# Softmax division behind the value product, as rows of reciprocals, and a transposed copy shared by two engines

## What is computed

```python
q = jnp.einsum('bpd,hdk->bphk', x, W_Q)      # 32 query heads, 8 key heads, d_head 64
k = jnp.einsum('bpd,ndk->bpnk', x, W_K)
v = jnp.einsum('bpd,ndk->bpnk', x, W_V)
gq = q.reshape(b, s, n_kv, g, d_head).transpose(0, 1, 3, 2, 4)
scores = jnp.einsum('bqgnh,bknh->bnqk', gq, k) / jnp.sqrt(jnp.float32(d_head))
scores = jnp.where(causal, IGNORE, scores)
pattern = jax.nn.softmax(scores, axis=-1)
z = jnp.einsum('bknh,bnqk->bqnh', v, pattern)
attn_out = jnp.einsum('bqnh,nhd->bqd', z, W_O)
```

## Time and profile before

| | us |
|---|---|
| median of 3 runs | 589.4 (585.45 to 589.74) |
| profiled execution | 584.7 |
| its span, first to last instruction | 582.9 |
| busy in it: PE / PEld | 512.2 / 418.7 |
| DVE / ACT / POOL | 380.2 / 287.3 / 158.1 |

### The profile page before, as it was taken

The page is one execution under the profiler, slowest core; times in us unless marked ns, Lnnn a source line. Parts: engine busy times, 40 slices in busy tenths (PEclk is TensorE's granted clock), DMA queues, the critical chain, the costliest instruction groups (busy, mean ns, idle before and its releaser), DMA issues. The chain is left out here.

```text
span 582.9 us, 9925 instructions
## 1 busy us (share of the span) xinstructions
PE 512.2 (88%) x3274; PEld 418.7 (72%) x3275; DVE 380.2 (65%) x964; ACT 287.3 (49%) x528; POOL 158.1 (27%) x205
## 2 busy tenths in 40 slices
PE   1996977899999999899989999717999999999994
PEld 1645865687797875666768778617888888998883
DVE  4896577746654736777777878455777666666661
ACT  1476353223502345465466656325666666666651
POOL 3703539402002202333223212110322222222222
PEclk9999999899998996899899999957999999999999
DMA  8997001000001009600000002941122222222211
GB/s 336 394 335 221 2 18 55 1 1 0 1 2 36 1 0 396 269 27 30 28 2 28 20 10 74 403 151 28 30 37 36 36 36 36 36 36 36 27 15 22
DMA packets 25780, 47.46 MB, mean 81 GB/s; under 512 B 2192, under 2 KB 21136, under 8 KB 25360
## 3 DMA queue, kind: packets, MB, share of 16 engines
q1 hardware_dynamic: 21232, 41.35, 19.8%
q0 software_dynamic: 4080, 5.15, 6.0%
q10 hardware_dynamic: 432, 0.49, 0.3%
HBM read 32.01 MB, written 14.98 MB: 81 GB/s over the span
## 5 line engine op out<-in xcount | busy, mean ns | idle before, releaser
L1602 PE MATMUL ps<-split,xsT 128*128 128x352 f32 x552 | 95.5, 330 | 0.8 <-DVE split L1244 0.8
L1602 PEld LDWEIGHTS ps<-split,xsT 128*128 128x128 f32 x552 | 89.5, 192 | 1.0 <-issue 1.0
L1244 DVE TENSOR_TENSOR split<-early,split 128x1408 fp32r<-128x1408 f32 x46 | 72.6, 1617 | 1.9 <-ACT split L783 1.9
L1624 PE MATMUL ps<-mid,work 128*128 (+1 forms) x276 | 67.9, 388 | 0.8 <-ACT work L772 0.8
L783 ACT CAST split<-early 128x1408 fp32r x46 | 62.6, 1365 | 0.8 <-issue 0.8
L1624 PEld LDWEIGHTS ps<-mid,work 128*128 128x128 f32 (+1 forms) x276 | 49.7, 189 | 13.4 <-issue 8.7
L1225 DVE TENSOR_TENSOR work<-work,ps 128x704 f32<-128x704 f32 x23 | 20.4, 886 | 56.4 <-PE ps L1602 56.4
L1114 DVE TENSOR_REDUCE nmax<-ps 128x1 f32<-128x128 f32 (+7 forms) x64 | 45.4, 750 | 7.3 <-PE ps L1508 7.2
L564 POOL TENSOR_TENSOR rstd<-mhalf 128x1 f32<-128x1 f32 x23 | 11.4, 494 | 138.3 <-ACT work L779 138.3
L1519 PE MATMUL ps<-cst,work 128*128 128x128 f32 x216 | 35.6, 293 | 4.8 <-DVE work L1122 2.8
L728 ACT COPY work<-ps 128x128 f32<-128x128 f32 (+7 forms) x32 | 20.6, 642 | 33.9 <-PE ps L1519 33.8
(11 more groups left out here) (250 smaller groups left out, 1118.1 us busy)
## 6 DMA issues: line engine op xcount, KB each, us to landing
early<-m_w SPq DMA_DIRECT2D x16, 704.0 KB, 10.1
expert_in<-pad SPq DMA_DIRECT2D x8, 1040.0 KB, 12.6
mid<-m_w SPq DMA_DIRECT2D x8, 640.0 KB, 8.5
work<-expert_in SPq DMA_DIRECT2D x23, 130.0 KB, 2.6
early<-factors SPq DMA_DIRECT2D x1, 2048.0 KB, 12.1
early<-wq SPq DMA_DIRECT2D x1, 2048.0 KB, 16.5
mid<-f_w SPq DMA_DIRECT2D x1, 2048.0 KB, 21.3
rows<-x_in SPq DMA_DIRECT2D x2, 512.0 KB, 4.9
```

Of the source, the lines that this page charges most:

```text
L1244: V.tensor_tensor(lo, (ew1, ew3)[w][:, bass.ds(e, 1), :], hi.bitcast(F32), ALU.subtract).then_inc(s_wlo[w], 1)
L1602: last = mm(ps[:, 2 * w + a, 0:IH], xsT[px][b][:, k, :], split_w[w][pw][:, k, a * IH:(a + 1) * IH], start=(k == 0 and px == pw), stop=(k = ...
L1624: last = mm(ps[:, 6, 0:D], eaT[0:w, b, c, :], we[0:w, c, :], start=(c == 0), stop=(c == IB - 1))
```

## The change

The exponentials are no longer divided by their sum. They are transposed and multiplied by v as they are, and the attended values, feature-major, are multiplied by rows that hold the reciprocals. VectorE takes the reciprocals of a tile's eight sums, copies each over 64 columns, TensorE transposes the four blocks of 128, ScalarE copies them to SBUF, and VectorE multiplies. In tiles 0 to 3 the transposes of the two heads of a step use bank 4 and bank 5 in turn, and ScalarE copies them whole. From tile 4 (WIDE = 32 heads) a row takes both banks; ScalarE copies the first 512 columns and VectorE the others, and the transposes of a step's first head come at the end of the step in which its exponentials are made. Attention output, routing transposes, counts, the choice of experts and the slots have other places in the orders, and the two new buffers take 1024 columns below k_hi, so that fewer parts of w3 are loaded early.

```diff
+        R_AT = K_AT - 2 * QB * P
+        inv_rows = early[:, R_AT:R_AT + QB * P]
+        inv_cols = early[:, R_AT + QB * P:K_AT]
+        WIDE = GT * HEADS
+        def pT_banks(u):
+            return 4 if u >= WIDE else 4 + u % 2
 # SP
-            early_w3 = (K_AT - E * KD * I) // (KD * I)
+            early_w3 = (R_AT - E * KD * I) // (KD * I)
+            below_k = -(-(K_AT - E * KD * I) // (KD * I))
...
-            for e in range(early_w3, E):
+            for e in range(below_k, E):
...
+            sp.wait_ge(s_zT, TT)
+            for e in range(early_w3, below_k):
+                sp.dma_start(ew3[:, e], m_w3[:, e]).then_inc(s_e13, 16)
             sp.wait_ge(s_pv, TT * HEADS // 2)
 # ScalarE
             def probs_feature_major(u):
-                w = (u // HEADS + 1) * P
+                w = min((u // HEADS + 1) * P, 512)
...
-            def z_feature_major(i):
+            def reciprocal_rows(i):
+                act.wait_ge(s_inv_tr, i + 1)
...
+                nc.scalar.copy(inv_rows, ps[:, 6 + (i + 1) % 2, :]).then_inc(s_inv, 1)
-            for m in range(STEPS + 7):
+            for m in range(STEPS + 6):
                 i, rel = divmod(m, PAIRS)
-                if rel == 2 and 1 <= i <= TT:
-                    z_feature_major(i - 1)
+                wide = 2 * m > WIDE
+                if rel == 1 and i >= 2:
+                    logits_exp(i - 2)
                 if 1 <= m <= STEPS:
                     probs_feature_major(2 * m - 2)
+                if rel == 2 and 1 <= i <= TT:
+                    reciprocal_rows(i - 1)
                 if rel == 0 and i >= 2:
                     routed_feature_major(i - 2)
-                if rel == 1 and i >= 2:
-                    logits_exp(i - 2)
+                if wide and m <= STEPS:
+                    probs_feature_major(2 * m - 1)
                 if m < STEPS:
                     attend(2 * m)
+                if 1 <= m and not wide:
+                    probs_feature_major(2 * m - 1)
+                if m < STEPS:
                     attend(2 * m + 1)
-                if 1 <= m <= STEPS:
-                    probs_feature_major(2 * m - 1)
 # VectorE
-            def normalised(u):
...
+            def probs_feature_major(u):
+                w = (u // HEADS + 1) * P - 512
+                dve.wait_ge(s_pt, u + 1)
+                dve.wait_ge(s_pv, u // 2 - 1)
+                V.tensor_copy(pT[u % 4][:, 512:512 + w], ps[:, 5, 0:w]).then_inc(s_pTv, 1)
+            def reciprocals(i):
+                dve.wait_ge(s_pr, (i + 1) * HEADS)
...
+                link(V.reciprocal(pinv[:, c], psums[:, c]))
+                V.tensor_copy(inv_cols.rearrange("p (n d) -> p n d", n=HEADS),
+                              pinv[:, c].unsqueeze(2).broadcast_to([P, HEADS, DH])).then_inc(s_pinv, 1)
+            def attended_normalised(i):
+                dve.wait_ge(s_inv, i + 1)
+                dve.wait_ge(s_pv, (i + 1) * PAIRS)
...
+                V.tensor_tensor(zT.rearrange("p a b -> p (a b)"), ps[:, 6 + i % 2, :], inv_rows,
+                                ALU.mult).then_inc(s_zT, 1)
...
-            for m in range(STEPS + 7):
+            for m in range(STEPS + 6):
                 i, rel = divmod(m, PAIRS)
-                if rel == 2 and i >= 2:
-                    route_slots(i - 2)
+                wide = WIDE < 2 * m <= 2 * STEPS
+                if wide:
+                    probs_feature_major(2 * m - 2)
+                if rel == 0 and i >= 2:
+                    route_normalise(i - 2)
                 if rel == 1 and i >= 2:
-                    route_max(i - 2)
-                if 1 <= m <= STEPS:
-                    normalised(2 * m - 2)
-                    normalised(2 * m - 1)
+                    route_choice(i - 2)
+                if m < STEPS:
+                    row_max(2 * m)
+                    row_max(2 * m + 1)
+                if wide:
+                    probs_feature_major(2 * m - 1)
+                if rel == 0 and 1 <= i <= TT:
+                    reciprocals(i - 1)
+                if rel == 2 and 1 <= i <= TT:
+                    attended_normalised(i - 1)
                 if rel == 3 and 1 <= i <= TT:
                     add_attention(i - 1)
                     route_variance(i - 1)
-                if m < STEPS:
-                    row_max(2 * m)
-                    row_max(2 * m + 1)
-                if rel == 3 and 1 <= i <= TT:
-                    route_normalise(i - 1)
+                if rel == 0 and i >= 2:
+                    route_max(i - 2)
                 if rel == 1 and i >= 2:
-                    route_choice(i - 2)
                     route_tail(i - 2)
+                    route_slots(i - 2)
 # TensorE
             def probs_transposed(u):
-                pe.wait_ge(s_pn, u + 1)
-                if u >= 1:
+                pe.wait_ge(s_pr, u + 1)
+                if u >= WIDE:
                     pe.wait_ge(s_pT, u)
+                    if u > WIDE:
+                        pe.wait_ge(s_pTv, u - WIDE)
+                elif u >= 2:
+                    pe.wait_ge(s_pT, u - 1)
...
             def attended(m):
+                if 2 * m >= WIDE:
+                    pe.wait_ge(s_pTv, 2 * m + 2 - WIDE)
-                if pair == 0 and i >= 2:
-                    pe.wait_ge(s_slots, i - 1)
+                if pair == 0 and i >= 1:
+                    pe.wait_ge(s_inv, i)
...
+            def reciprocals_transposed(i):
+                pe.wait_ge(s_pinv, i + 1)
+                if i >= 1:
+                    pe.wait_ge(s_cnt_read, i)
+                for pair in range(PAIRS):
+                    last = nc.tensor.transpose(ps[:, 6 + (i + 1) % 2, pair * P:(pair + 1) * P],
+                                               inv_cols[:, pair * P:(pair + 1) * P], ident)
+                last.then_inc(s_inv_tr, 1)
...
-                if 1 <= m <= STEPS:
-                    probs_transposed(2 * m - 2)
+                if rel == 2 and 1 <= i <= TT:
+                    reciprocals_transposed(i - 1)
+                if rel == 3 and 1 <= i <= TT:
+                    attention_out(i - 1)
                 if rel == 0 and i >= 2:
                     route_transposed(i - 2)
+                if 1 <= m <= WIDE // 2:
+                    probs_transposed(2 * m - 2)
+                if 1 <= m <= STEPS:
+                    probs_transposed(2 * m - 1)
+                if rel == 1 and i >= 2:
+                    route_counts(i - 2)
                 if 2 <= m <= STEPS + 1:
                     attended(m - 2)
-                if 1 <= m <= STEPS:
-                    probs_transposed(2 * m - 1)
-                if rel == 2 and 1 <= i <= TT:
-                    attention_out(i - 1)
                 if rel == 0 and i >= 2:
                     route_logits(i - 2)
-                if rel == 1 and i >= 2:
-                    route_counts(i - 2)
+                if WIDE // 2 <= m < STEPS:
+                    probs_transposed(2 * m)
```

30 lines of the change are left out of this document (14 added, 16 removed).

## The result

| | before | after |
|---|---|---|
| median of 20 runs each, us | 589.51 (584.38 to 590.88) | 584.96 (578.95 to 591.89) |
| ratio, 95% interval | | 0.9923 (0.9896 to 0.9950) |
| profiled execution / its span | 584.7 / 582.9 | 581.0 / 579.2 |
| mean granted clock of it | 0.957 | 0.972 |

The forecast was 1.4 us slower; the kernel became about 4.5 us faster, 0.8% by the ratio. Ratios leave out the runs that are over 1.5% above the fastest of their kernel, six of these twenty of the changed kernel and none of before, while medians and means take all: the means of the twenty are 588.0 and 585.3, so the gain is 0.5% by the means.

A forecast was written before the change was run, and what follows sets the result against it. TensorE was taken as the attention stage's bound, at 92%. Stage before its tail -1.3 and tail +2.7 sum to +1.4: 586.1 us on the profiled 584.7, 590.8 on the median 589.4; range 582.5 to 597.

The forecast's parts named there:

- tile 1, "+1.2": Tile 1: no idle time to give, +0.4 or +0.9 for added transposes by clock, plus the reciprocal-row wait: +1.2 us.
- rival (2): Clock rises in tile 1, whose 14.08 us hold 8.3 of work at 2.4 GHz: up to -5.8, about 585; chance 0.12.
- of the 2.0 us that TensorE idles I give back 1.3: Tile 3, tile 2 the same: 1.3 of 2.0 us TensorE idle time returns, the rest being counts that still wait.
- the wait for the reciprocal rows: Tiles 1 to 3: a tile's first value product waits for ScalarE's copy of the reciprocal rows, 0.75 us.
- four steps at "about 0.1": Tile 4: the split copy cuts about 0.1 us a step, against 0.43 for transposes and the dearer output; taken as 0.
- the steps forecast at 6.0, 6.2 and 6.2: Tile 7's steps with routing transposes and logits (6.0 us), choice of experts (6.2) and reciprocals (6.2).
- The tail: After the last exponential: routing transposes +0.25, counts before the last value product +1.2, reciprocals and product behind it +1.3; together +2.7.
- SP's late loads: Two of eight w3 loads move behind the last normalised values; costed at nothing, 1 to 4 us if stores queue behind.
- a rival at +2 to +4: Late w3 loads do collide: +2 to +4 us, 593 to 595; chance 0.08.
- The fifth rival: VectorE's part is slower still, maxima and PSUM copies in one queue, 0.2 in each of 16 steps: +3.2, 594; chance 0.07.
- The first, all waits gone: TensorE never waits in the attention stage: -6.9 us, 582.5; chance 0.15.
- The third, low clock through tiles 2 and 3: Clock stays at 1.2 GHz through tile 2 or 3 too; one more such tile costs 5.8 us, 596.6; chance 0.13.

The follow-up runs named there:

- after_held: Changed kernel with tile 0's old wait put back: VectorE takes an unread reciprocal, scales rows by 1.0, transposes wait for it; 593.58 us, ratio to before 1.0058.
- before_filler: Kernel before plus thirteen unread 256-column matmuls, 9 and 4 around the first transposes of tile 0; 581.14 us, ratio 0.9900.
- no_norm: Kernel before without the division: no reciprocals or scalings, transposes wait for the exponentials alone, output not the softmax; 583.15 us, ratio 0.9883.
- ao_later: Changed kernel with the attention output placed behind the second head's transposes; one run, tiles 3 to 6 shorter by 0.51, 0.44, 0.41 and 0.30 us.
- tail: Changed kernel, reordered behind the last exponential: reciprocal transposes before the last value product, tile 6's counts after it, VectorE's product before the slots; 587.44 us, ratio 0.9868.
- tail_loads: Kernel tail with other homes for the two new buffers and tile 6's store no longer ahead of the late w3 loads; 584.06 us, ratio to before 0.9864.
- whole_copy: Changed kernel with ScalarE copying the whole transposed row in tiles 4 to 7; one run, tiles 4, 5, 6 longer by 0.30, 0.72 and 0.90 us.
- after_filler: Changed kernel plus unread 256-column matmuls where TensorE stands, 4 in tile 0 and the others in the tail and before the experts; 582.16 us.

## Why the prediction was wrong

**The step that failed** is tile 1, "+1.2", and behind it the weight of rival (2). The sum took tile 1 to be at 1.2 GHz as before, and the trace of the kernel after shows 1.00 and 10.28 us: -3.8. The median by rival (2) was to be "about 585", and it is 584.96. I gave it 0.12. That the two agree so well is luck: the rival took 5.8 us off tile 1, the trace 3.8, and twelve of the twenty runs have more low clock than the traced one. The prediction named the fact that pointed to it, the 1.22 and 0.45 us for which TensorE stood in tile 0 just ahead of the fall, and costed the removal of that stand at its own length only. after_held and before_filler show the link from both sides. no_norm does not settle which part of the change matters: with VectorE's wait gone, but the 0.45 behind ScalarE's copy still there, the clock fell, but it fell as well in ao_later, tail and tail_loads, which have the changed tile 0, and all four traces had the lower clock ahead of attention. Whether the two banks in tile 0 matter beside the division is open; the banks alone were not tried. Even in the changed kernel twelve of twenty runs have more low clock than the eight best. The gain is thus one of odds. 46.8 us of low clock on the mean against some 60 are 13 x 0.315 = 4.2 us, less 1.8 of structure: -2.4. The means of the 20 runs each are 588.0 and 585.3, a difference of 2.7. The 4.5 between the medians is more than that because of where each lies in its upper group.

**The structure, at equal clock.** before_filler gives the tiles of before at full clock, so the terms can be laid side by side: tile 0 -1.2 (forecast -1.2), tile 1 +0.6 (+1.2), tile 2 +0.5 (-0.1), tile 3 +0.7 (-0.1), tile 4 -1.2 (0; in part clock, see below), tile 5 -0.6 (-0.3), tile 6 -0.4 (-0.4), tile 7 -0.3 (-0.4). Together -1.9, where -1.3 was forecast; without the clock's part in tile 4 it is an estimated -0.5. Misses of both signs partly cancel.

- Tiles 2 and 3: "of the 2.0 us that TensorE idles I give back 1.3" was wrong. The counts still wait 1.0 and 0.7 us there, and 1.05 us of wait before the first wide scores (ScalarE puts a copy between the two exponentials that they need, at 264.28) was not seen. That wait could have been read off the diff: the last narrow step has the narrow order, but the scores behind it already want wide banks.
- Tile 1: the wait for the reciprocal rows is 0.8 as forecast (0.75), but the prediction added the doubled cost of the transposes at 1.2 GHz.
- Tile 4: both traces of the order before have 3.4 us at 1.2 GHz in it, and no_norm, at full clock, took 19.93. With the 0.4 to 0.6 that the division costs in the tiles beside it, tile 4 of before would be some 20.4 at full clock, an estimate; then the changed order is 0.3 longer there and the clock accounts for about 1.5. whole_copy gives the split copy 0.3 in the tile; four steps at "about 0.1" were to be 0.4.
- Tiles 5 to 7 came out as worked: 5.88, 6.23 and 6.30 us for the steps forecast at 6.0, 6.2 and 6.2. VectorE's copy of 512 columns takes 0.69 us, the value taken from L1110, and releases the second transposes. The rule of the Trainium skill weighed there (VectorE: DVE Perf Modes, section "Why PSUM operands drop a tier"), that a PSUM operand costs VectorE its fast pass, fits: 688 ns for 512 columns from PSUM, beside 753 for 1024 in SBUF. It did not decide, since whole_copy shows the split to gain 2.6 us all the same; the freed ScalarE pays for it.

**The tail** was forecast at +2.9 from the last exponential to the residual add (13.9 against 11.03) and measured at +4.3, 1.2 of it the clock. Order and places were right: a last value product behind the counts with 2.2 us of wait (forecast "some 2"), then transposes, copy and product. Up to the first expert product it is +3.8, where the sum had +2.7. The stage's -0.5 and these 3.8, less the 1.2 of clock, make 2.1, near the 1.8 found at equal clock.

**SP's late loads** were costed at nothing, with a rival at +2 to +4. In the changed kernel they are just level with the table; once the tail is shorter they take its whole gain, as tail shows. The sum over stages hides this: two chains end at the experts, and shortening one of them alone gives nothing.

**The fifth rival**, a slower VectorE, is out by the steps of tile 7. The first, all waits gone, is out by the counts. The third, low clock through tiles 2 and 3 for the stand ahead of the value product, is not seen: in every trace with the changed orders tile 2 is at 0.90 or more and tile 3 at 1.00.

## What to carry to other kernels

Where the trace shows TensorE at 1.2 GHz in a full stretch, read what it did just before, and price a removed or added stand there by the tile that follows as well as by its own length: here 1.22 us of standing went with 4.4 us in the next tile. Look at the low clock of every run before trusting a median, since it can sit at the edge of one of two groups, and compare orders at equal clock; one trace of a kernel can show the good case alone. When a chain is shortened, ask which other chain ends at the same place; here the transfers for the next stage and then the first rows behind the table.

## What the runs showed of the hardware

- Fifty to 67 us of each run of before were at 1.2 GHz, in the trace in stretches of 3.4 to 20.5 us, over a kernel in which TensorE is busy for 512 of 583 us. At 0.315 us each that is 16 to 21 us, some 3% of the time. The Trainium skill (TensorE: Matmul & The Clock Gate, section "What's actually happening") puts the ramp at under 1% of a typical kernel; here the fall recurs in the middle and costs, by this estimate, three times that. Its section "HAM oscillation — how this bites in real kernels" ties such falls to waits for transfers between bursts of matmuls; after_held and before_filler agree that a stand can bring the fall, but here it is one of 1.22 us, shorter than the waits in that section's case, and for another engine.
- The price of low clock depends on the place: some 5 us for a stretch of 13.65 in tiles 0 and 1 (before against before_filler); in the tail 13.8 us less of it gave 1.0 us at the table and 0.7 in the first expert products (after_filler), and the start of the experts did not come earlier for it.
- Thirteen unread matmuls in one place made the kernel before 1% faster; a hundred made the changed kernel steady (2.4 us between the extremes in place of 13), 1.4 us below the median that four of them gave.
- The changed kernel's low clock went from 29 to 70 us between runs of one program. In the traces, part of the difference lies ahead of attention: 0.97 or 0.88 to 0.89 from 49 to 112.5 us, with the same work. What decides that from run to run the runs do not show.
